# An R-GCN layer on one Trainium2 core: a quarter of the edge tiles by counted dense products instead of gathers

## What is computed

```python
def _rgcn_layer(x, W, SW, b, src, dst, rel):
    xt = jnp.einsum('nd,rde->rne', x, W)
    msg = xt[rel, src]
    agg = jax.ops.segment_sum(msg, dst, num_segments=x.shape[0])
    return jax.nn.relu(agg + x @ SW + b)
x = _rgcn_layer(entity_emb, w1, sl1, b1, src, dst, edge_type)
x = _rgcn_layer(x, w2, sl2, b2, src, dst, edge_type)
```

## Time and profile before

| | us |
|---|---|
| median of 3 runs (4266.47 to 4269.35) | 4267.82 |
| span of the profiled execution | 4266.3 |
| PE busy | 3043.3 (71%) |
| VectorE busy | 2017.8 (47%) |
| ScalarE busy | 705.0 (17%) |
| POOL busy | 2364.9 (55%) |
| L574, gathers of both passes, 1612 | 1534.2, 0.952 each |
| L602, their products, 3224 records | 1254.7 |

### The profile page before, as it was taken

One profiled execution on the slowest core, in us unless ns is written; L12 is line 12 of the kernel. 1 busy time (PEld: TensorE's weight loads), 2 busy tenths in 40 slices (PEclk: granted clock), 3 DMA queues, 4 the chain that ended last, 5 costly groups with the idle time before them and its releaser, 6 DMA issues.

```text
span 4266.3 us, 42581 instructions
## 1 busy us (share of the span) xinstructions
PE 3043.3 (71%) x12281; PEld 2000.6 (47%) x12281; DVE 2017.8 (47%) x4124; ACT 705.0 (17%) x1923; POOL 2364.9 (55%) x2466
## 2 busy tenths in 40 slices
PE   5666798996888888888376666666667666666666
PEld 3555454554666666565243333333344333433334
DVE  7777685467988888898631111111112111111112
ACT  2334201002444444343320000000001000000000
POOL 3000000004777777776237777777775777777776
PEclk8778898998999999899675555555557555555555
DMA  3544754463444444443041111111123111111112
GB/s 125 214 191 194 302 215 190 200 263 97 119 115 114 118 110 118 110 118 97 3 149 53 53 53 53 53 53 52 53 70 142 53 53 53 52 53 53 52 53 63
DMA packets 236740, 456.14 MB, mean 107 GB/s; under 512 B 64036, under 2 KB 183570, under 8 KB 231392
## 3 DMA queue, kind: packets, MB, share of 16 engines
q1 hardware_dynamic: 158728, 291.44, 18.8%
q0 software_dynamic: 77792, 161.98, 13.9%
HBM read 336.68 MB, written 116.51 MB: 106 GB/s over the span
## 4 chain that ended last, share of the span: by engine, by line
POOL 37%; PE 26%; issue 17%; DMA 15%; DVE 4%; ACT 2%; SPq 0%; ACTq 0%; DVEq 0%; POOLq 0%
POOL edge_buffers L574 21%; POOL round_buffers L1124 16%; DMA edge_buffers<-rel_table,relidx 13%; PE sums L794 9%; PE sums L602 4%; PE sums L706 3%; PE sums L702 3%; PE sums L1582 2%; PE sums L711 1%; ACT adj_window L737 0%; DMA adj<-adj_window 0%; ACT chunk_and_window L737 0%; DMA adj_chunk<-adj 0%; PE sums L1246 0%; DVE tile_moments L487 0%
## 5 line engine op out<-in xcount | busy, mean ns | idle before, releaser
L574 POOL DMA_INDIRECT edge_buffers<-rel_table,relidx x1612 | 1534.2, 952 | 586.0 <-PE sums L602 268.8
L602 PE MATMUL sums<-edge_buffers 128*128 128x128 f32 x3224 | 1254.7, 495 | 750.2 <-DMA edge_buffers<-rel_table,relidx 746.4
L602 PEld LDWEIGHTS sums<-edge_buffers 128*128 128x128 f32 x3224 | 802.1, 310 | 1206.0 <-issue 1205.1
L585 DVE TENSOR_SCALAR edge_buffers<-iota,rel 128x128 f32<-128x128 f32 x1612 | 335.2, 296 | 1644.4 <-PE sums L602 1644.4
L1124 POOL DMA_INDIRECT round_buffers<-xs_t,srcs x806 | 765.5, 950 | 570.9 <-DMA xd_t<-round_buffers 325.5
L631 ACT ACTIVATE trio<-sums,c_L_b 128x256 f32<-128x256 f32 (+1 forms) x16 | 8.0, 500 | 2020.4 <-PE sums L606 2020.4
L944 POOL IOTA trio<- 128x806 int32 x1 | 0.8, 805 | 603.8 <-ACT H L517 603.8
L1168 PE MATMUL sums<-round_buffers,ident 128*128 128x408 f32 x620 | 278.6, 533 | 27.6 <-DMA round_buffers<-xs_t,srcs 24.1
L1171 PEld LDWEIGHTS sums<-round_buffers 128*128 128x128 f32 x1612 | 243.5, 198 | 76.1 <-issue 65.6
L1268 ACT ACTIVATE trio<-sums 128x128 f32 x806 | 223.7, 278 | 279.7 <-PE sums L1246 196.7
L1171 PE MATMUL sums<-round_buffers 128*128 128x136 f32 x1612 | 244.8, 285 | 0.0
(11 more groups left out here) (289 smaller groups left out, 3000.0 us busy)
## 6 DMA issues: line engine op xcount, KB each, us to landing
chunk_and_window<-adj SPq DMA_DIRECT2D x10, 5600.0 KB, 15.8
round_buffers<-xd_t SPq DMA_DIRECT2D x806, 68.0 KB
adj_chunk<-adj SPq DMA_DIRECT2D x9, 5600.0 KB, 16.5
adj<-adj_window SPq DMA_DIRECT2D x11, 3850.0 KB, 11.5
...
edge_buffers<-rel_table,relidx POOLq DMA_INDIRECT x1612, 2.5
...
round_buffers<-xs_t,srcs POOLq DMA_INDIRECT x806, 2.5
```

The lines of the kernel that those rows point to most:

```text
L574: nc.gpsimd.indirect_dma_start(slot(t), None, table[:, :], bass.IndirectOffsetOnAxis(ap=index[:, t:t + 1], axis=0)).then_inc(slot_sem(t), 16)
L585: made = nc.vector.tensor_scalar(round_hots(i)[:, k, :], iota[:, :], rel[:, t:t + 1], None, ALU.is_equal)
L602: nc.tensor.matmul(sums[:, bass.ds(place[k], P)], slot(t), round_hots(i)[:, k, :], start=False, stop=False).then_inc(summed_n, 1)
```

## The change

In each relation pass 195 consecutive edge tiles (LT) of the 806 are no longer gathered. The kernel chooses the range of tiles on the chip, one of four (PICKS), by the fewest nodes it spans, and takes it out of the lists of table rows, destinations and places (`choose_range`, `leave_range_out`, on VectorE near L1475); 611 tiles in 47 rounds (IG) stay.

For the edges of the range, "steps" are built, each the meeting of one tile and one destination node: S = 988 in NW = 38 windows of SW = 26. In the first pass ScalarE spreads, for 13 steps at a time, each edge's source (node modulo 128, and node over 128 with the relation: 25 x 8 = 200) over 128 + 200 columns in float16; VectorE compares them with a row of numbers held in PSUM; TensorE multiplies the one-hots (128 edges, 128 by 200), which counts the step's edges by source and relation; ScalarE moves two steps' counts (400 columns) out of PSUM, and SyncE stores each window (26 x 200 numbers in each of 128 partitions) to DRAM. The second pass loads the counts back. In both passes a window's counts are multiplied by the node features H (25 products of 26 x 8 = 208 columns, float32), ScalarE moves the result, and after four windows 8 products by the relation weights and one by a one-hot bring the sums to their nodes.

The banks no longer accumulate. Tiles are summed in groups of 4, 3, 3 and 3 into two PSUM banks in turn, each product by itself, and VectorE adds each to B1T in SBUF at an address from a register, each add waiting for the one before. B1T starts with the own product (`own_product`). The compare of a round becomes one instruction with the row of numbers in PSUM. The schedules of the engines are written out: in STEP_AT 40 of the first 45 rounds get a window number. The diff, its core (not shown: the building of the step lists between the tables and the first pass, some 40 small operations on VectorE, TensorE and ScalarE, the second pass's VectorE and ScalarE schedules, which leave the step work out, the products of the window rows, and the new source arrays):

```diff
@@ -41,6 +41,22 @@
 BANKS = 8
 LAST_TILE = [(E - N + STRIDE * (j + 1) - 1) // P for j in range(BANKS - 1)] + [ET - 1]
+LT, PICKS = 195, 4
+GT = ET - LT
+IG = GT // U
+SPAN = (N + PICKS - 1) // PICKS
+SW, NW = 26, 38
+S = SW * NW
+SH = S // 2
+RUN = SW // 2
+WT = 4
+SP_ = SW * WT
+NWT = -(-NW // WT)
+GROUPS = ((0, 4), (4, 7), (7, 10), (10, U))
+TAIL = IG - 2
+STEP_AT = {1 + v * 43 // 39: v for v in range(NW + 2)}
+CLOSE_AT = [t - LT for t in LAST_TILE]
+TAIL_GROUPS = [(TAIL * U, CLOSE_AT[0] - 2)] + [(t - 2, t + 1) for t in CLOSE_AT]
...
-        def sum_in_banks(table, index, ready, at_close):
...
+        choose_range()
+        listed = leave_range_out(relidx[:, 0:ET])
+        leave_range_out(rel[:, 0:ET])
+        V.did(V.after().tensor_scalar(nodes.rearrange("p (i k) -> p i k", k=U), d0row[0:1, 0:IT, 0:U], float(LASTFIRST),
+                                      None, ALU.min))
+        leave_range_out(nodes)
+        V.did(V.after().tensor_copy(offrow[0:1, 0:IG, 0:U], nodes[:, 0:GT].rearrange("p (i k) -> p i k", k=U)))
...
+        def own_product(w):
+            for c in range(NCH):
+                b = 4 + c % 4
+                T.need(last_evac[b])
+                s = slice(c * CH, (c + 1) * CH)
+                m = T.did(nc.tensor.matmul(pb[b][:, 0:CH], Wt[w][:, :], HT[:, s], start=True, stop=True))
+                A.need(m)
+                last_evac[b] = A.did(nc.scalar.activation(B1T[:, s], pb[b][:, 0:CH], ACT.Copy))
+            return A.now()
...
+        def gather_rows(p, ready):
+            for mark in ready:
+                nc.gpsimd.wait_ge(*mark)
+            for i in range(IG):
+                for k in range(U):
+                    t = (p * IG + i) * U + k
+                    nc.gpsimd.wait_ge(summed_n, START + max(0, t - 2 * U + 1))
+                    nc.gpsimd.indirect_dma_start(
+                        slot(p * IG + i, k), None, rel_t[p][:, :],
+                        bass.IndirectOffsetOnAxis(ap=relidx[:, i * U + k:i * U + k + 1], axis=0)
+                    ).then_inc(slot_sem(p * IG + i, k), 16)
+        def wait_for_part(g):
+            if g > 1:
+                nc.tensor.wait_ge(added_n, put[g - 1])
+        def sum_tiles(p, i, lo, hi):
+            q, g = p * IG + i, len(put) - 1
+            wait_for_part(g)
+            nc.tensor.wait_ge(hots_n, START + q + 1)
+            for k in range(lo, hi):
+                nc.tensor.wait_ge(slot_sem(q, k), 16 * (q // 2 + 1))
+                nc.tensor.matmul(part_of(g)[:, (k - lo) * P:(k - lo + 1) * P], slot(q, k), round_hots(q)[:, k, :],
+                                 start=True, stop=True).then_inc(summed_n, 1)
+            put.append(put[-1] + hi - lo)
+        def count_steps(w, half):
+            nc.tensor.wait_ge(onehot_n, 2 * w + half + 1)
+            for k in range(RUN):
+                s = half * RUN + k
+                q = w * RUN + s // 2
+                if s % 2 == 0 and q >= 3:
+                    nc.tensor.wait_ge(evict_n, q - 2)
+                m = nc.tensor.matmul(pb[q % 3][:, s % 2 * HR:(s % 2 + 1) * HR], ehot[:, half, k, 0:P],
+                                     ehot[:, half, k, P:P + HR], start=True, stop=True)
+                if s % 2:
+                    m.then_inc(step_n, 1)
+            if half == 0:
+                m.then_inc(used_n, 1)
+        def window_product(p, w, lo, hi):
+            z = p * NW + w
+            if lo == 0:
+                if p == 0:
+                    nc.tensor.wait_ge(evict_n, RUN * (w + 1))
+                else:
+                    nc.tensor.wait_ge(s_load[w % 2], 16 * (w // 2 + 1))
+                if z:
+                    nc.tensor.wait_ge(zout_n, z)
+            for h in range(lo, hi):
+                m = nc.tensor.matmul(pb[4][:, 0:SW * R].rearrange("p (s r) -> p s r", r=R), H[:, h, :],
+                                     counts[:, w % 2, :, h * R:(h + 1) * R], start=(h == 0), stop=(h == HI - 1))
+            if hi == HI:
+                m.then_inc(dense_n, 1)
...
+        def tensor_of_first():
+            for i in range(TAIL):
+                v = STEP_AT.get(i, NW + 9)
+                sum_tiles(0, i, *GROUPS[0])
+                if v < NW:
+                    count_steps(v, 0)
+                if last_of_pair(v - 2):
+                    rows_of_pairs(0, (v - 2) // WT)
+                sum_tiles(0, i, *GROUPS[1])
+                if v < NW:
+                    count_steps(v, 1)
+                if last_of_pair(v - 2):
+                    sum_pairs(0, (v - 2) // WT)
+                sum_tiles(0, i, *GROUPS[2])
+                if 1 <= v <= NW:
+                    window_product(0, v - 1, 0, RUN)
+                sum_tiles(0, i, *GROUPS[3])
+                if 1 <= v <= NW:
+                    window_product(0, v - 1, RUN, HI)
+        def tensor_of_second():
+            for i in range(TAIL):
+                v = STEP_AT.get(i, NW + 9)
+                sum_tiles(1, i, *GROUPS[0])
+                if last_of_pair(v - 1):
+                    rows_of_pairs(1, (v - 1) // WT)
+                sum_tiles(1, i, *GROUPS[1])
+                if v < NW:
+                    window_product(1, v, 0, RUN)
+                if last_of_pair(v - 1):
+                    sum_pairs(1, (v - 1) // WT)
+                sum_tiles(1, i, *GROUPS[2])
+                if v < NW:
+                    window_product(1, v, RUN, HI)
+                sum_tiles(1, i, *GROUPS[3])
+        def compare_round(p, i):
+            q = p * IG + i
+            if q > 1:
+                nc.vector.wait_ge(summed_n, START + (q - 1) * U)
+            nc.vector.tensor_tensor(round_hots(q), pb[3][:, 0:P].unsqueeze(1).to_broadcast([P, U, P]),
+                                    rel[:, i * U:(i + 1) * U].unsqueeze(2).to_broadcast([P, U, P]),
+                                    ALU.is_equal).then_inc(hots_n, 1)
+        def compare_steps(w, half):
+            nc.vector.wait_ge(bcast_n, 2 * w + half + 1)
+            nc.vector.tensor_tensor(ehot[:, half], numbers.unsqueeze(1).to_broadcast([P, RUN, P + HR]), ehot[:, half],
+                                    ALU.is_equal).then_inc(onehot_n, 1)
+        def places(row, lo, hi):
+            return nc.values_load_multi_w_load_instructions(
+                row[:, lo:hi], engines=(ENG.DVE,), min_val=0, max_val=LASTFIRST,
+                skip_runtime_bounds_check_because="clamped on the chip")[1]
+        def add_sum(g, j, place):
+            if taken[-1] + j:
+                nc.vector.wait_ge(added_n, taken[-1] + j)
+            held = B1T[:, bass.ds(place, P)]
+            nc.vector.tensor_tensor(held, held, part_of(g)[:, j * P:(j + 1) * P], ALU.add).then_inc(added_n, 1)
+        def add_tiles(p, i, lo, hi, place):
+            g = len(taken) - 1
+            nc.vector.wait_ge(summed_n, START + (p * IG + i) * U + hi)
+            for k in range(lo, hi):
+                add_sum(g, k - lo, place[k - lo])
+            taken.append(taken[-1] + hi - lo)
...
+        def vector_of_first():
+            compare_steps(0, 0)
+            compare_steps(0, 1)
+            for i in range(TAIL):
+                v = STEP_AT.get(i, NW + 9)
+                compare_round(0, i + 1)
+                place = places(offrow[0:1, i, :], 0, U)
+                for lo, hi in GROUPS[0:2]:
+                    add_tiles(0, i, lo, hi, place[lo:hi])
+                if v + 1 < NW:
+                    compare_steps(v + 1, 0)
+                if last_of_pair(v - 2):
+                    add_pairs(0, (v - 2) // WT)
+                add_tiles(0, i, *GROUPS[2], place[GROUPS[2][0]:GROUPS[2][1]])
+                if v + 1 < NW:
+                    compare_steps(v + 1, 1)
+                add_tiles(0, i, *GROUPS[3], place[GROUPS[3][0]:GROUPS[3][1]])
...
+        def spread_steps(w, half):
+            if w:
+                nc.scalar.wait_ge(*((step_n, RUN * w) if half else (used_n, w)))
+            s = w * SW + half * RUN
+            nc.scalar.activation(ehot[:, half, :, 0:P], steplo[:, s:s + RUN].unsqueeze(2).to_broadcast([P, RUN, P]), ACT.Copy)
+            nc.scalar.activation(ehot[:, half, :, P:P + HR], stephr[:, s:s + RUN].unsqueeze(2).to_broadcast([P, RUN, HR]),
+                                 ACT.Copy).then_inc(bcast_n, 1)
+        def move_counts(w, lo, hi):
+            if lo == 0 and w > 1:
+                nc.scalar.wait_ge(dense_n, w - 1)
+                nc.scalar.wait_ge(s_cnt[w % 2], 16 * (w // 2))
+            for j in range(lo, hi):
+                q = w * RUN + j
+                nc.scalar.wait_ge(step_n, q + 1)
+                nc.scalar.activation(counts[:, w % 2, 2 * j:2 * j + 2, :].rearrange("p s c -> p (s c)"),
+                                     pb[q % 3][:, 0:2 * HR], ACT.Copy).then_inc(evict_n, 1)
+        def move_window_sums(p, w):
+            k = p * NWT + w // WT
+            nc.scalar.wait_ge(dense_n, p * NW + w + 1)
+            if w % WT == 0 and k > 1:
+                nc.scalar.wait_ge(prow_n, k - 1)
```

(66 more changed lines are left out.)

334 lines of the change are left out of this document (248 added, 86 removed).

## The result

| us | before | after |
|---|---|---|
| median | 4267.15 (4262.43 to 4269.35) | 3917.26 (3913.24 to 3920.01, 4 runs) |
| span of the profiled execution | 4266.3 | 3918.6 |
| pass 1, first to last gather's start | 1011.5 | 904.7 |
| pass 2, the same | 1011.5 | 762.3 |
| from the last gather's start to the end | 11.2 | 11.8 |

The ratio is 0.9184, 95% interval 0.9171 to 0.9197. The prediction said 3955, range 3840 to 4170: right, and 38 us too high. The page of the profile after, read beside the earlier trace rows, shows a clock of 8 to 9 in the passes' slices where 5 stood, and PE leads the chain.

A forecast was written before the change was run, and what follows sets the result against it. Gathers at 1.2555 us a tile bound both passes before; afterwards PE and ScalarE pace pass 1 at 22.4 a round. Second pass from 3179, plus 761 for 611 gathers, plus 11.1, 2 and 1.5, gave 3955 us, range 3840 to 4170.

The forecast's parts named there:

- the surcharge in 1.2555: Gathers beside 13 compares take 0.99 and 1.06 us, not 0.94; one PSUM-operand compare gives 1.246 a tile, 5 us a pass.
- The round of pass 1: Pass 1, one round with a window: 22.4 us, paced by PE and ScalarE, not by the gathers' 16.2.
- the clock's term: Pass 1 round: at clock 0.93 the five parts after the count steps (11.45 us) cost 0.9 more.
- The 0.8 us for hand-overs between engines: Pass 1 round: some six hand-overs between engines of 0.13 us each, taking 21.6 to 22.4.
- The rows of pairs: Products by the relation weights after four windows: counted at 0.6 us per window of PE work in pass 2.
- The start: Before pass 1: tables end near 2190, own product 5.4 us, step lists 17, spreads and compare; round 1 at about 2230.
- the range choice: Range choice and compaction of three lists: some 11 us on VectorE, costed at nothing inside its 11.98 us wait for the scatter.
- Between the passes: First closing to the second pass's first gather: 55 us instead of 59.5, as table products alternate four banks from the start.
- The VectorE rival: VectorE bounds pass 1, a round of 26 us, 4090 in all; chance 0.26 for VectorE or more hand-overs (4030 to 4200).
- Gathers as the bound of pass 1: Gathers stay the bound in pass 1 too, a round of 17.9 us or less, 3770 in all; chance 0.08.
- No gathers dropped: Both passes would keep 1.25 x 806 if 195 gathers were not dropped; dismissed since the loop runs over 47 rounds.
- The clock at half: Granted clock stays at 0.50: about 4660 us, or 4345 in pass 1 alone; low clock chance 0.11, 0.09 slower than before.

The follow-up runs named there:

- the last experiment: Changed kernel with the row of numbers for the round and step compares in SBUF instead of PSUM: 4838.30 us beside the changed kernel's 4832.71.
- the second group: Runs on one chip: changed kernel 4722.45 us, ScalarE's evictions before both spreads 4675.07, 23 of 25 window products left out 4659.19, more VectorE compares 4718.73.
- the third: Runs on one chip: changed kernel 4832.71 us, ScalarE's and VectorE's orders turned 4781.36, six products among count steps besides 4788.76, numbers in SBUF 4838.30.

## Why the prediction was right, and where it was off

**Pass 2** was sized within 2 us: 610 steps between gathers at 1.2497 us (1.246 said), tail 11.8 (13.1). The larger part of the surcharge in 1.2555 went with the 13 compares; the last experiment shows the like of it, a gather held up beside VectorE.

**The round of pass 1** was said to be 22.4 and was 20.8. By its own parts: the 26 steps end 8.8 us after their start (2575.99 to 2583.09 + 1.70), 9.25 said, as evictions follow each other after 0.38 to 0.40 instead of 0.45. The rest, 2563.83 to 2575.99, is 12.2 us, where 11.45 and 0.9 for the clock, 12.35 in all, were said. So the clock's term came near by luck: a mean clock over all products was said, and the price lies in the 16 products right behind the wait (0.70 + 0.47 = 1.2 us here, 1.4 with the median's 5.41), while the others run at full clock. The 0.8 us for hand-overs between engines is the term that had nothing to stand for: the sum that follows the steps comes to 21.6 without it, and the measured round is below even that (0.45 by the steps, 0.2 by the rest, and 0.2 as the last count steps overlap the first tile product). The rows of pairs had been left out of the round: with them a window takes 23.0 to 23.6 us in eight cases, and in a ninth, which has no spread any more, 18.3. Against 22.4 each, the 36 windows come to 27 x -1.6 + 8 x 0.7 - 4 = -42 us.

**The start** was 8 us late: the first count step began at 2238.1 instead of round 1 at 2230. 2.4 of it stand already where the scaled pieces begin, at 2088.01 instead of 2085.59. Only 1.1 of these belong to the range choice, which the prediction hid in VectorE's wait of 11.98 us: it filled the wait, and the scatters of GpSimd beside it took longer. The other 1.3 came before it, as the scatters started at 2066.90 instead of 2065.56:

```profile
2079.27 0.80 DVE L1453 TENSOR_TENSOR round_buffers<-round_buffers 128x611 f32<-128x611 f32 x1
2080.10 0.80 DVE L1454 TENSOR_TENSOR relidx<-relidx,round_buffers 128x611 int32<-128x611 int32 x1
2080.38 1.36 POOL L1413 DMA_INDIRECT scale_t<-positive,piece_column  x1 [0.30 <-issue]
...
2088.01 4.76 DVE L1468 TENSOR_TENSOR round_buffers<-round_buffers,positive 128x384 f32<-128x384 f32 x4 [0.75 <-DMA positive<-scale_t]
```

The larger part is the step lists: from the end of the own product (2198.9, 2195.4 said) to the first tile product (2221.86) it took 23.0 us instead of 17. The two step compares after it took 2.4 us each and not 4.6.

**Between the passes.** The first closing came at 3087.2 instead of 3124: +8 - 42, and 3 less, in part by the rounds without a window (some 6.3 us by three of them, 7 said). From there to the second pass's first gather it took 57.3 us (55 said):

```profile
3087.19 0.61 ACT L2035 ACTIVATE trio<-trio,c_L_b 128x384 f32<-128x384 f32 x1 [10.93 <-DVE trio L1875]
...
3144.46 0.94 POOL L1752 DMA_INDIRECT edge_buffers<-rel_table,relidx  x1 [41.11 <-DMA rel_table<-table_stages]
...
3906.80 0.94 POOL L1752 DMA_INDIRECT edge_buffers<-rel_table,relidx  x1 [0.30 <-PE sums L2003]
```

That is 3144.5 for a predicted 3179, and these 34.5 us are nearly all of the 38. They are the difference of errors that partly cancel: rounds too dear by 45 us, a start and a stretch between the passes too cheap by 10. The rest is that the median lies 1.3 us under the profiled span and not 1.5 above.

**Single prices**, said and measured: tile product 0.28 and 0.28 (three in 0.83); window product 0.35 and 0.37 (12 in 4.39); count step 0.11 and 0.11 (six in 0.68); spreads 4.0 and 4.05; round compare 1.88 and 1.88; add 0.32 and 0.43 from one to the next (three in 1.15), hidden; step compare 4.6 and 2.38, hidden. The last was the wrong choice between two rows, the float32 one with PSUM and the float16 one in SBUF: the type sets the pace, 0.56 ns an element from either memory. The Trainium skill (VectorE: DVE Perf Modes, The perf-mode tier table) led the same way with 1x for any PSUM operand; the measurement decides against it. The VectorE rival lived on this price.

**The rivals.** Gathers as the bound of pass 1: no, 1.53 us each there. VectorE: no, by the run with more of its work. No gathers dropped: no, there are 1222 instead of 1612. The clock at half: no, 0.91 and 0.89 in the windows. That last one had a true core: with window products gone, the second pass's clock fell to 0.61 between 3930 and 4700 us, where the changed kernel on the same chip had 0.83 (the clock is the third number from the end):

```profile
3930.00:4700.00 770.00, 307.84 (x1347) 262.13 (x1347) 226.18 (x579) 26.40 (x50) 470.04 (x497) 0.61 0.44 152
```

**A version that beats both** is the changed kernel with ScalarE's order turned: 47 us less in the second group. With VectorE's order turned too it was 51 less in the third. Both are from chips with holes; on one like the result's neither was run.
